# A recommender kernel: TensorE's extra semaphore waits moved onto the weight loads of second and third products

## What is computed

```python
e = jnp.stack([tbl_0[ids[:, 0]], tbl_1[ids[:, 1]], ... ], axis=1)      # 1024 x 39 x 16
for W in [f0, f1, f2]:                                                  # 1521x128, 4992x128, 4992x128
    z = jnp.einsum('bfd,bgd->bfgd', x0, xk).reshape(b, f * g, d)
    cur = jnp.einsum('bpd,pm->bmd', z, W)
    outs.append(cur)
    xk = cur
z = jnp.sum(jnp.concatenate(outs, axis=1), axis=-1)
h = jnp.concatenate([z, dense_ctx], axis=1)
h = jnp.maximum(h @ W_top1 + b_top1, 0.0)
h = jnp.maximum(h @ W_top2 + b_top2, 0.0)
y = h @ W_top3
```

## Time and profile before

| | us |
|---|---|
| median of 3 runs | 1272.41 (1269.62 to 1273.38) |
| the profiled execution | 1262.4 |
| its span | 1260.6 |
| PE busy | 1230.0 (98%) |
| DVE / ACT / POOL busy | 1080.0 / 983.5 / 964.8 |

### The profile page before, as it was taken

One profiled execution on the slowest core, in us unless ns is written; L12 is line 12 of the kernel. 1 busy time (PEld: TensorE's weight loads), 2 busy tenths in 40 slices (PEclk: granted clock), 3 DMA queues, 4 the chain that ended last, 5 costly groups with the idle time before them and its releaser, 6 DMA issues.

```text
span 1260.6 us, 23302 instructions
## 1 busy us (share of the span) xinstructions
PE 1230.0 (98%) x6037; PEld 1014.7 (80%) x6037; DVE 1080.0 (86%) x3370; ACT 983.5 (78%) x3272; POOL 964.8 (77%) x745
## 2 busy tenths in 40 slices
PE   3999999999999999999999999999999999999998
PEld 2677788888888888888888888888888888888887
DVE  3889999789988899789997899978999789988884
ACT  2678887788877888778886888868888688877883
POOL 7788888688886788777887778867888678884462
PEclk9999999999999999999999999999999999999999
DMA  6484343323433323334331433313433223343000
GB/s 157 97 220 92 85 87 84 59 59 63 85 86 80 69 62 70 68 83 83 72 78 34 85 82 86 80 34 68 85 86 84 63 48 70 85 86 76 9 6 4
DMA packets 159563, 94.76 MB, mean 75 GB/s; under 512 B 114385, under 2 KB 122065, under 8 KB 159430
## 3 DMA queue, kind: packets, MB, share of 16 engines
q1 hardware_dynamic: 149190, 90.63, 32.5%
q0 software_dynamic: 10240, 2.64, 2.4%
HBM read 84.08 MB, written 3.87 MB: 70 GB/s over the span
## 4 chain that ended last, share of the span: by engine, by line
PE 94%; DVE 3%; issue 1%; POOL 1%; ACT 1%; DMA 0%; SPq 0%; DVEq 0%; ACTq 0%; POOLq 0%
PE pieces L867 23%; PE pieces L869 22%; PE pieces L868 22%; PE cur_bank L895 6%; PE cur_bank L851 4%; PE cur_bank L849 4%; PE cur_bank L850 3%; DVE parts L658 2%; PE gx_bank L883 1%; PE gx_bank L884 1%; PE gx_bank L885 1%; PE cur_bank L921 1%; PE gx_bank L821 1%; POOL emb L407 1%; PE pieces L938 1%
## 5 line engine op out<-in xcount | busy, mean ns | idle before, releaser
L481 ACT ACTIVATE parts<-pieces,x_cols 128x128 f32<-128x128 f32 x2560 | 723.5, 374 | 138.9 <-PE pieces L869 132.3
L658 DVE SCALAR_TENSOR_TENSOR parts<-pieces,x_cols,parts 128x128 f32<-128x128 f32 x2432 | 683.6, 344 | 139.8 <-PE pieces L869 118.5
L867 PE MATMUL pieces<-w_hi,cur_hi 128*128 128x512 f32 (+1 forms) x1280 | 514.8, 402 | 4.6 <-issue 2.4
L869 PE MATMUL pieces<-w_hi,cur_lo 128*128 128x512 f32 (+1 forms) x1280 | 498.5, 389 | 0.0
L868 PE MATMUL pieces<-w_lo,cur_hi 128*128 128x512 f32 (+1 forms) x1280 | 498.3, 389 | 0.0
L416 POOL TENSOR_TENSOR parts<-parts 128x1024 f32<-128x1024 f32 x127 | 305.4, 2404 | 159.7 <-DVE parts L658 156.9
L407 POOL DMA_INDIRECT emb<-in_table,rows x320 | 318.3, 995 | 81.8 <-issue 58.4
L867 PEld LDWEIGHTS pieces<-w_hi,cur_hi 128*128 128x128 f32 x1280 | 241.4, 189 | 56.5 <-DVE parts L658 6.8
L869 PEld LDWEIGHTS pieces<-w_hi,cur_lo 128*128 128x128 f32 x1280 | 240.9, 188 | 51.7
L868 PEld LDWEIGHTS pieces<-w_lo,cur_hi 128*128 128x128 f32 x1280 | 241.4, 189 | 40.0
L421 POOL TENSOR_TENSOR tails<-parts 128x512 f32<-128x512 f32 x127 | 164.2, 1293 | 18.1
(11 more groups left out here) (99 smaller groups left out, 835.6 us busy)
## 6 DMA issues: line engine op xcount, KB each, us to landing
partners<-x_wide SPq DMA_DIRECT2D x186, 234.0 KB
x_diag<-x_split SPq DMA_DIRECT2D x512, 10.0 KB
x_end<-x_wide SPq DMA_DIRECT2D x96, 80.0 KB
x_rep<-x_wide SPq DMA_DIRECT2D x96, 78.0 KB
partners<-x_wide SPq DMA_DIRECT2D x93, 80.0 KB
emb<-in_table,rows POOLq DMA_INDIRECT x320
partners<-x_wide SPq DMA_DIRECT2D x62, 66.0 KB
x_wide<-emb SPq DMA_DIRECT2D x32, 80.0 KB
```

The costliest lines, as they stand in the source:

```text
L481: last = nc.scalar.activation(parts[n % 2][:, 4 * i + r, :], src[:, r * H:(r + 1) * H], ACT.Copy, scale=x_cols[n // 4][:, n % 4, f:f + 1])
L658: nc.vector.scalar_tensor_tensor(acc, src[:, r * H:(r + 1) * H], x_cols[n // 4][:, n % 4, f:f + 1], acc, ALU.mult, ALU.add).then_inc(acc_d ...
L867: nc.tensor.matmul(dst[:, 0:width], hi[:, cols], w1_hi[:, ws], start=True, stop=False)
L869: nc.tensor.matmul(dst[:, 0:width], lo[:, cols], w1_hi[:, ws], start=False, stop=True).then_inc(l2d_ready if q in D_PIECES else l2a_ready, 1)
```

## The change

Only TensorE's program is changed; the matmuls and their order stay the same.

- Waits that another wait implies are left out (`cur1_hi_ready` and mostly `cur1_lo_ready` beside `sum1_ready`, `g_copied` and others repeated ahead of a group).
- `layer2_piece` is split into its three products. The remaining waits of a short group, all but one, are put on the second and third product of a piece ahead of it: the step just ahead for `transpose_x`, `sum_pairs`, `layer3`, `top1`, `top2`, `top3`; the same step's own piece for `make_g`.
- In particular the wait for the bank being read (`await_bank_read`) goes to the third product of the piece at `s == steps.sum[0] - 1`, one step ahead of the first `sum_pairs`.
- The wait for the next tile's `cur1_lo` goes to the third product of the tile's last piece.

```diff
             def sum_pairs(tile, i, k):
                 g, buf, rows = tile * PAIRK + k, (i * PAIRK + k) % 2, rows_of(k)
                 pe.wait_ge(pairs_lo_ready, g + 1)
-                if k == 0:
-                    wait(pe, cur1_lo_ready, tile)
-                    wait(pe, sum1_ready, tile)
-                    if i == 1:
-                        wait(pe, y_copied, tile // TILES - 1)
-                    if i == 2:
-                        wait(pe, l3_copied, tile // TILES)
-                    if i == 3:
-                        wait(pe, h1_copied, tile // TILES * 2)
-                    if i == TILES:
-                        wait(pe, h2_copied, tile // TILES - 1)
...
+            def await_bank_read(tile, i):
+                if i == 1:
+                    wait(pe, y_copied, tile // TILES - 1)
+                if i == 2:
+                    wait(pe, l3_copied, tile // TILES)
+                if i == 3:
+                    wait(pe, h1_copied, tile // TILES * 2)
+                if i == TILES:
+                    wait(pe, h2_copied, tile // TILES - 1)
...
-                pe.wait_ge(x_cols_ready, turned)
-                if n % 2 == 0:
-                    tile = u * TILES + n // 4
-                    pe.wait_ge(x_diag_loaded[n // 2 % 2], (tile + 1) * 16 * DIAG_LOADS)
-                wait(pe, g_copied, g)
...
                 if step == 0:
-                    pe.wait_ge(top_loaded, 7 * 16)
-                    pe.wait_ge(g_copied, (u + 1) * BLOCKS)
-                    pe.wait_ge(cur1_lo_ready, tiles)
                     pe.wait_ge(sum1_ready, tiles)
...
-                    pe.wait_ge(cur1_hi_ready, tile + 1)
-                    pe.wait_ge(cur1_lo_ready, tile + 1)
+                    if tile <= 1:
+                        pe.wait_ge(cur1_lo_ready, tile + 1)
...
+                        layer2_first(u, n, q)
+
+                        if more and s == S_X - 1:
+                            pe.wait_ge(x_rep_loaded[(i + 1) % 2], (tile + 1 - (i + 1) % 2) * 8 * X_LOADS + 16 * X_LOADS)
+                        if more and s == steps.sum[0] - 1:
+                            await_last_sum(tile + 1)
+                        if g_next:
+                            await_diag(next_u - next_back, next_b)
+                        if g_now:
+                            pe.wait_ge(x_cols_ready, x_turned(u, at))
+                        if not first and at == S_L3[0] - 1:
+                            pe.wait_ge(g_copied, u * BLOCKS)
...
+                        layer2_second(n, q)
+
+                        if more and s == S_X - 1:
+                            pe.wait_ge(x_cols_ready, tile + 1)
+                        if more and s == steps.sum[0] - 1:
+                            await_bank_read(tile + 1, i + 1)
+                        if g_now:
+                            wait(pe, g_copied, (u - back) * BLOCKS + b)
...
+                        if more and tile > 0 and s == 4 * PIECES - 1:
+                            pe.wait_ge(cur1_lo_ready, tile + 2)
+                        layer2_third(n, q)
```

More of the change, by code:

```diff
@@ L852, in sum_pairs, with await_last_sum, piece_of, layer2_first @@
                                  ).then_inc(pairs_used, 1)
-            def layer2_piece(u, n, q):
-                width = min(4, F - 4 * q) * H
-                dst = pieces[(n * PIECES + q) % BANKS]
+            def await_last_sum(tile):
+                wait(pe, sum1_ready, tile)
+            def await_bank_read(tile, i):
[7 more added lines that the diff above has]
+                    wait(pe, h2_copied, tile // TILES - 1)
+            def piece_of(n, q):
+                width = min(4, F - 4 * q) * H
+                dst = pieces[(n * PIECES + q) % BANKS][:, 0:width]
+                lo, hi = cur1_lo[n // 4 % 2], cur1_hi[n // 4 % 2]
+                cols = slice(n % 4 * P, (n % 4 + 1) * P)
+                return dst, hi[:, cols], lo[:, cols], slice(4 * q * H, 4 * q * H + width)
+            def layer2_first(u, n, q):
                 g, back = (u * BLOCKS + n, q - BANKS) if q >= BANKS else (u * BLOCKS + n - 1, q - BANKS + PIECES)
@@ L946, in _ @@
                 if k == 1:
+                    pe.wait_ge(x_rep_loaded[0], 16 * X_LOADS)
                     transpose_x(0, 0, 0)
@@ L963, in quad @@
                         at = 4 * PIECES * i + s
-                        layer2_piece(u, n, q)
+                        steps = S_BEGIN if first and i == 0 else S_USUAL
+                        back, b = G_STEP.get(at, (0, 0))
+                        g_now = at in G_STEP and u >= back
+                        next_back, next_b = G_STEP.get((at + 1) % (BLOCKS * PIECES), (0, 0))
+                        next_u = u + (at + 1) // (BLOCKS * PIECES)
+                        g_next = (at + 1) % (BLOCKS * PIECES) in G_STEP and next_u >= next_back and next_u < QUADS
@@ new lines, in quad @@
+                        if not first and at == S_L3[0] - 1:
+                            pe.wait_ge(g_copied, u * BLOCKS)
+                        if not first and at == S_H1[0] - 1:
+                            pe.wait_ge(l3_copied, u)
+                        if not first and at == S_H2[0] - 1:
+                            pe.wait_ge(h1_copied, u * 2)
+                        if not first and at == S_Y - 1:
+                            pe.wait_ge(h2_copied, u)
+                        layer2_second(n, q)
@@ L965, in quad @@
+                        layer2_third(n, q)
                         if more and s == S_X:
                             transpose_x(tile + 1, (i + 1) % TILES, g_made(u, at))
-                        steps = S_BEGIN if first and i == 0 else S_USUAL
                         if more and s in steps.sum:
                             sum_pairs(tile + 1, i + 1, steps.sum.index(s))
-                        if at in G_STEP:
-                            back, b = G_STEP[at]
-                            if u >= back:
-                                make_g(u - back, b, x_turned(u, at))
+                        if g_now:
+                            make_g(u - back, b)
@@ L990, in _ @@
             pe.wait_ge(sum1_ready, QUADS * TILES)
-            make_g(u, BLOCKS - 4)
-            make_g(u, BLOCKS - 3)
-            make_g(u, BLOCKS - 2)
+            pe.wait_ge(x_cols_ready, QUADS * TILES)
+            for n in range(BLOCKS - 4, BLOCKS - 1):
+                await_diag(u, n)
+                pe.wait_ge(g_copied, u * BLOCKS + n)
+                make_g(u, n)
             warm_up(3, x_bank)
```

38 lines of the change are left out of this document (19 added, 19 removed).

## The result

| | before | after |
|---|---|---|
| median of 6 runs, us | 1272.89 (1269.62 to 1274.17) | 1280.05 (1277.37 to 1281.35) |
| ratio of the medians | | 1.0064 [1.0052, 1.0076] |
| the profiled execution, us | 1262.4 | 1279.94 |
| its span, us | 1260.6 | 1278.1 |

The change costs 7.2 us, 0.64%. Forecast were +7.1 us and 1279.5.

A forecast was written before the change was run, and what follows sets the result against it. TensorE's queue was taken to bound the kernel. An early wait at +8.8 us and sum1 waits without steps at -1.7 gave +7.1, so 1272.4 became 1279.5 us, with an 8-in-10 range of 1271 to 1286.

The forecast's parts named there:

- TensorE's queue is the time: Whole kernel: TensorE is busy 1230.0 of 1260.6 us, so only what stretches or shortens its queue counts.
- Part 1: Step 49's third product waits early for ACT's third-layer copy: 1.25 us in each of seven quads, +8.8 us.
- Nothing is given back: Later waits in each quad shift with the step 49 pause, so nothing is subtracted from the +8.8 us.
- The second rival: Later waits of the quad hide behind the step 49 pause, or the copy comes sooner: +0.8 us, 1273.2; 15%.
- Part 2: At 7 x 4 groups needing sum1, the late wait moves from step to load, gaining 0.06 us each: -1.7 us.
- Part 3: Other waits placed earlier are met in time: cost 0, perhaps +0.2 to +0.5 us once in the first quad.
- Wait steps are free in the shade: TensorE's sequencer does satisfied wait steps behind streaming products, so removing 334 of 51 ns moves nothing; opposing rival 7%.
- The clock: Rival: TensorE's clock falls behind each of seven step 49 pauses, 1.4 us each, giving 1289.3 us; 6%.
- The carrying over from one profiled execution to the median: The 10.0 us by which the median exceeds the profiled execution is kept: 1269.5 us profiled, 1279.5 us median.

The follow-up runs named there:

- e10: Changed kernel with ACT's copy L544 cut into 32 slices of 4 columns, semaphore on the last; 1307.52 us, ratio 1.0289.
- e2: Kernel before with only the l3_copied wait moved, to the third product of step 49; 1279.94 us, ratio 1.0068.
- e5: Kernel before; layer3, top1, top2, top3 keep only the sum1 wait, on the load, their others moved ahead or dropped; 1269.82 us, ratio 0.9995.
- e1: Changed kernel with the l3_copied wait put back ahead of the first product of tile 2's sum; 1270.16 us, ratio 0.9990.
- e4: As e1, with ACT's third-layer copy one step sooner, right behind the weighing of piece 48; 1266.85 us, ratio 0.9969.
- e7: Kernel before without any edit, profiled a second time; 1269.56 us in that one execution.
- e11: The same kernel as e4, measured again against other runs of the kernel before; 1267.95 us, ratio 0.9976.
- e3: Kernel before with three long-satisfied waits ahead of every piece's second product, 1280 more wait steps; 1270.89 us, ratio 0.9997.

## Why the prediction was right

- *TensorE's queue is the time.* Held: everything measured here is the sum of what lengthens or shortens that queue, from -0.06 us at one group to +1.53 at step 49, and in e10 the slower clock on top.
- *Part 1, +8.8 us.* Held: +1.53 at step 49 and -0.29 at step 50, 1.24 a quad for the 1.25 of the working; alone (e2) +8.5 us. L877 waits seven times, 1.58 us for the load and 1.26 for the products, and the sum's wait is gone.
- *Nothing is given back.* Held. From step 50 to the next quad's step 49 the shift stays but for the three gains of part 2 and the two values of the third layer. The later waits of the quad, on ACT at step 90 and on the sums, are still there: they hang on TensorE's own earlier products and move with them. The second rival is out.
- *Part 2, -1.7 us.* Its mechanism held and its size was too large: 0.05 us from release to load where 0.12 stood before, but in three groups of a quad and not in four, 21 x 0.063 = 1.3 us. The fourth, at step 159, was counted in with the others from the totals of the earlier trace rows, where L931 has 1.7 us against 1.2; the prediction shows no timeline of it, and there the sum is ready before the load comes up. In the median of e5 alone even the 1.3 us do not rise above the scatter. That +7.1 us meets the +7.2 of the medians so closely is luck: with the first quad's 0.2 us (next point) the parts as measured give 8.7 - 1.3 + 0.2 = 7.6 us, which the interval of the ratio, 6.6 to 9.7 us, holds as well.
- *Part 3, nothing.* Held: e1, which has parts 2 and 3, and e5, with part 2 alone, differ by no more than 0.04 us at any step of a steady quad. The first quad does hold one of these waits, as allowed for. At its step 53 the third product waits for ACT's copy of G, which ends at 93.55 + 0.46 = 94.01 in e4, and its load starts at 94.06. Three pairs of traces, with and without the moved waits (e4 and e7, e11 and e2, e10 and e5), differ by 0.18 to 0.19 us at this step. It is the mechanism of part 1 in small, once. The load in e4:

```profile
94.06 0.19 PEld L877 LDWEIGHTS pieces<-w_hi,cur_lo 128*128 128x128 f32 x1 [0.54 <-issue]
```

- *Wait steps are free in the shade.* Held, now with 1280 more of them (e3), where the trace of before had shown one place. That place was read a little wrong: the step at 536.9 stands four loads ahead of its `make_g` and not two products, so the sequencer's lead is larger than I wrote.
- *The clock.* Held at 1.3 us at this place. The price of 1.4 us for a fall was too low: it came from a half-clock stretch of 3.5 us, and six of e10's seven are 6.8 us long. The pause at 1233 us of the earlier trace rows, behind which the clock stayed, was weaker evidence than I took it for: in e7 the clock fell a few us behind the same pause.
- *The carrying over from one profiled execution to the median.* It held because the difference of 10.0 us was taken over whole. The profiled execution of after, 1279.94, is not the 1269.5 that the sum gave for it: the quick start of the first trace did not come again, in any of the profiles taken later. The median was the safer ground, and whoever compares the two profiled times sees 17.5 us, of which 10.4 aren't the change's.

## What to carry to other kernels

In these runs a wait that has been met costs nothing wherever it stands, in a step of its own or on a load; so moving waits off the short groups can gain only where a semaphore arrives last, and there 0.06 us. A wait that has not been met costs all that its semaphore is late at the new place, and everything in the queue behind it pays: before a wait is moved up, read from the trace when its semaphore is raised and when the new carrier starts. If there is a real wait at the old place, let the engine that raises it do that work sooner (here -0.29 us a quad); and keep pauses of TensorE short: behind those of 3.2 us the clock cost another 2 to 2.5 us each, and behind several short ones close together it fell in 8 traces of 13. Compare kernels over their steady part, or by medians, and not by two profiled executions.

## What the runs showed of the hardware that I had not expected

- 1280 instructions of 51 ns in TensorE's own queue, one per piece, moved the time by less than could be measured (0.9997 [0.9983, 1.0011]).
- A small ACT copy queued behind another of its kind adds only 0.06 us (eight slices 0.73 us, one whole copy 0.30). I had expected nearly three times that.
- TensorE kept 2.4 GHz through seven pauses of 1.3 us and seven of 1.7 us, and fell to 1.2 GHz behind each of seven pauses of 3.2 us, for 3.4 us once and 6.8 us six times. At half clock a 512-wide product took 0.43 us instead of 0.23. But behind one pause of 2.35 us, and behind four of 0.6 to 1.4 us within 8 us, it fell in one execution and not in another of the same kernel.
- Two executions of one and the same kernel differ by 5.5 us in the start and by 1.6 us in the tail, where the clock fell in one of them, and so by 7.2 in the profiled time, while the steady quads agree to the hundredth.
